# Scattering the first three batches' rows in groups of two instead of four, in a routed feed-forward kernel

## The chip, the cores and the metric

The kernel runs on one core of one Trainium2 chip. The metric is the device time of one launch, in microseconds (us). Names of engines: PE is TensorE, DVE is VectorE, ACT is ScalarE, POOL is GpSimd, SP is SyncE, whose queue issues most of the plain transfers.

## The reference, cut to what matters

```python
x = x + layernorm(attn(layernorm(x)))      # x is (4, 1024, 256)
x = x + layernorm(ffn(layernorm(x)))

# attn: q, k projections, rotary, exp of causal scores, row sums, then a small two-layer map
# ffn, on the 4096 rows "flat":
logits = flat @ gate_w + gate_b            # 8 experts
topv, topi = lax.top_k(logits, 2)
topw = softmax(topv)                       # two weights per row
for each expert e:                         # w1[e]: 256 x 1024, w2[e]: 1024 x 256
    h = gelu(flat @ w1[e] + b1[e])
    final += (h @ w2[e] + b2[e]) * routing[:, e]
```

Every row goes to two of eight experts. The kernel computes only those two.

## The kernel before, in words

The attention part works batch by batch, four batches (B) of 1024 rows. While batch j + 1 is in the attention part, batch j is routed: the gate's logits, the two best experts and each row's place are computed (`choose`, `rank`, `place_rows`), and the rows are scattered into a DRAM table `sorted_x`, in which each expert has a region of its own. Rows lie on 128 partitions, 8 tiles (TB) to a batch, and each goes to two experts, so a batch is sent by 16 indirect transfers of 128 rows of 260 floats (133 KB) each. `send_rows` (L190, the transfer on L195) issues them on POOL, and every one adds 16 to the semaphore `rows_sent`.

After the attention part come the tiles of 256 rows of one expert each: SP loads a tile `xt` from `sorted_x`, PE turns it, multiplies it by the first layer (L838 for the tiles worked ahead, L1638 in the main loop), ACT takes the GELU, DVE splits the result in two parts, PE does the second layer (L845, L1651), and POOL adds the rows to the DRAM sum `sum_y` (L542). Matrices are split in a high and a low part, so each product is three matmuls.

What sets the order around the change:

- POOL's program is in order. For the batches 0 to 2 it waits for `rows_ready` of that batch (given by DVE, L1161), issues the 16 transfers in groups of `BURST`, waits (`hold`, L75) before each further group until all the ones ahead have landed, and after the last group waits for its landing too, and gives `rows_left` (L569 to L575). The last batch (L580 to L587) is sent in portions that are a list of its own, `SEND_FIRST`, between the additions to `sum_y` of the first two tiles.
- SP's queue issues the weights of the first two experts as soon as the busiest expert is known (L524 to L530, 4 transfers of 1 MB), and then waits until batches 0 and 1 are wholly landed, `rows_sent` at 2 batches (L531), and loads the first two tiles (L536). These are worked ahead, amid the last batch's attention part.
- PE's program has `turn_ahead(0)` (L824, which waits for the first tile) ahead of `attention_mlp(3)` (L806, L815) and of the first layer of that tile (L838). Before `turn_ahead(0)` stand 14 matmuls of `keep_warm` (L748), which compute nothing that is used. DVE too has `save_tag(0)` (L473), which waits for the first tile, ahead of `hidden(3)` (L1012 to L1021).
- Every later tile waits until batches 0 to 2 have landed, and some until all four have (L1487).
- DVE waits for `rows_left` of batch 0 at L1155 (batch 2's places) and L1334, and for that of batch 1 at L1155 (batch 3's places) and L1359.

Of the kernel before, what the change touches and what calls it, by code (L numbers as in the profile page):

```python
# [58 lines left out]
SP_ENDS = 4  # L59
END_SENT = NE * 16  # L60
SEND_FIRST = (6, 8, 11)
BURST = 4


RSQRT_LINKS = 8
# [9 lines left out]
def hold(eng, sem, value, passed):  # L75

    eng.wait_ge(sem, value)
    eng.sem_inc(passed, 1)
# [48 lines left out]
def build(nc, x_in, wqT, wkT, fc1_w, fc1_b, fc2_wT, fc2_b, low_rows, gate_w, gate_b, w1, b1T, w2, b2,  # L127
# [7 lines left out]
    with ExitStack() as ctx:  # L135
# [54 lines left out]
        def send_rows(pool, c, which):  # L190

            rows = xrow_last if c == B - 1 else xrows[:, c * TB:(c + 1) * TB, :]
            for i in which:
                at = c % 2 * 2 * TB + i
                pool.indirect_dma_start(  # L195
                    out=sorted_x, out_offset=bass.IndirectOffsetOnAxis(ap=slot_i[:, at:at + 1], axis=0),
                    in_=rows[:, i % TB, :], in_offset=None).then_inc(rows_sent, 16)
# [350 lines left out]
        def _(pool):  # L548
# [20 lines left out]
            for b in range(B - 1):  # L569
                pool.wait_ge(rows_ready, b + 1)  # L570
                for first in range(0, 2 * TB, BURST):
                    if first > 0:
                        hold(pool, rows_sent, b * BATCH_SENT + first * 16, passed)
                    send_rows(pool, b, range(first, first + BURST))
                hold(pool, rows_sent, (b + 1) * BATCH_SENT, rows_left)  # L575
# [1287 lines left out]
```

## Time and profile before

| | |
|---|---|
| median of 3 runs | 625.47 us (624.44 to 625.89) |
| the profiled execution, its own time | 628.62 us |
| its span, first to last instruction | 626.8 us |
| PE busy | 559.9 us (89%) |
| DVE busy | 415.6 us (66%) |
| ACT busy | 366.1 us (58%) |
| POOL busy | 182.6 us (29%) |
| mean granted clock of TensorE | 0.982 of full speed |

The busy shares are averages over a program with two unlike parts: up to about 195 us the attention part and the routing, from there to about 603 us the loop over expert tiles, in which PE is nearly always busy. Times in the rows below are counted from the span's start. The indirect transfers show twice: the instruction on POOL that issues one (about 1 us of POOL), and its landing, which shows only in who waited for it.

### The profile page before, as it was taken

How to read it: one execution, taken by the hardware profiler on the slowest of the kernel's cores; microseconds unless marked ns; L12 is line 12 of the kernel's file. 1: busy time of each engine (PE TensorE's matmuls, PEld its weight loads, DVE VectorE, ACT ScalarE, POOL GpSimd, SP SyncE). 2: the span in 40 equal slices, each digit the busy share in tenths (PEclk: the TensorE clock that was granted, in tenths of full speed). 3: DMA queues.
4: the chain of work that ended last, by engine and by line, in shares of the span. 5: the costliest groups of instructions: out<-in, count | busy, mean ns of one | idle time of the engine just before them, and what ended most of it. 6: DMA issues, size and time to landing. Idle time of an engine off the chain costs nothing.

```text
span 626.8 us, 14745 instructions
## 1 busy us (share of the span) xinstructions
PE 559.9 (89%) x4306; PEld 499.4 (80%) x4307; DVE 415.6 (66%) x1293; ACT 366.1 (58%) x836; POOL 182.6 (29%) x153
## 2 busy tenths in 40 slices
PE   2988998987998899999999999899999999999940
PEld 1747373644668899999999989899999999998940
DVE  4789698987987555455554556486489655455476
ACT  4376677774644453644635565684688654553582
POOL 2000054355536622313214213113212312312320
PEclk9999999999999989999999999999999999999985
DMA  8930011633227732323322263473473422322479
GB/s 221 359 127 0 2 69 69 237 136 111 73 101 191 225 51 51 50 34 54 47 43 50 43 170 61 93 244 58 70 235 81 67 36 51 50 34 51 89 201 330
DMA packets 51869, 66.80 MB, mean 107 GB/s; under 512 B 4886, under 2 KB 45308, under 8 KB 51708
## 3 DMA queue, kind: packets, MB, share of 16 engines
q1 hardware_dynamic: 37820, 47.87, 24.2%
q0 software_dynamic: 14016, 18.56, 17.2%
q8 instruction: 12, 0.20, 0.1%
q14 instruction: 21, 0.17, 0.1%
HBM read 38.26 MB, written 28.74 MB: 107 GB/s over the span
## 4 chain that ended last, share of the span: by engine, by line
PE 73%; DVE 9%; ACT 5%; issue 4%; DMA 4%; POOL 2%; another core or an unknown queue 1%; DVEq 1%; SPq 0%; ACTq 0%; POOLq 0%
PE pY L1651 30%; PE pL L1638 28%; PE pP L778 5%; DMA sorted_x<-xrows,slot_i 2%; PE pX L464 2%; DVE z L1795 2%; POOL sorted_x L195 2%; PE pP L881 2%; PE pS L795 2%; ACT probs L666 1%; PE pP L838 1%; PE pT L759 1%; ACT xn L597 1%; DMA x_all<-x 1%
## 5 line engine op out<-in xcount | busy, mean ns | idle before, releaser
L1573 ACT ACTIVATE h<-pL,b_now 128x256 f32<-128x256 f32 x272 | 112.6, 465 | 153.7 <-PE pL L1638 80.8
L542 POOL DMA_INDIRECT sum_y<-y,dest x68 | 107.0, 1573 | 274.8 <-DVE y L1695 262.4
L1668 DVE TENSOR_TENSOR h_lo<-h,h_hi 128x512 fp32r<-128x512 f32 x136 | 93.2, 692 | 112.8 <-ACT h_hi L1579 112.2
L1638 PE MATMUL pL<-xeT_hi,w_lo 128*128 128x256 f32 x544 | 151.6, 279 | 6.5 <-issue 5.7
L1651 PE MATMUL pY<-w_hi,h_lo 128*128 128x256 f32 x544 | 155.1, 285 | 2.5 <-DVE h_lo L1668 1.5
L1651 PE MATMUL pY<-w_hi,h_hi 128*128 128x256 f32 x544 | 151.6, 279 | 0.6 <-issue 0.6
L1651 PE MATMUL pY<-w_lo,h_hi 128*128 128x256 f32 x544 | 151.5, 279 | 0.5 <-issue 0.5
L1638 PE MATMUL pL<-xeT_lo,w_hi 128*128 128x256 f32 x544 | 151.0, 278 | 0.0
L1638 PE MATMUL pL<-xeT_hi,w_hi 128*128 128x256 f32 x544 | 150.9, 277 | 0.0
L1638 PEld LDWEIGHTS pL<-xeT_hi,w_lo 128*128 128x128 f32 x544 | 102.0, 188 | 7.8 <-issue 6.9
L1651 PEld LDWEIGHTS pY<-w_hi,h_lo 128*128 128x128 f32 x544 | 102.8, 189 | 4.5 <-DVE h_lo L1668 2.6
L1651 PEld LDWEIGHTS pY<-w_lo,h_hi 128*128 128x128 f32 x544 | 103.3, 190 | 0.5 <-issue 0.4
L1651 PEld LDWEIGHTS pY<-w_hi,h_hi 128*128 128x128 f32 x544 | 102.9, 189 | 0.4 <-issue 0.4
L1638 PEld LDWEIGHTS pL<-xeT_hi,w_hi 128*128 128x128 f32 x544 | 102.1, 188 | 0.1
L1638 PEld LDWEIGHTS pL<-xeT_lo,w_hi 128*128 128x128 f32 x544 | 102.1, 188 | 0.0
L1579 ACT ACTIVATE h_hi<-h 128x512 fp32r<-128x512 f32 x136 | 86.0, 632 | 6.3
L195 POOL DMA_INDIRECT sorted_x<-xrows,slot_i x48 | 49.1, 1023 | 120.0 <-DVE xrows L1161 82.3
L210 DVE TENSOR_TENSOR w_lo<-w_stage,w_hi 128x512 fp32r<-128x512 f32 x64 | 42.4, 686 | 15.0 <-issue 15.0
L1687 DVE SCALAR_TENSOR_TENSOR y<-pY,b_all 128x256 f32<-128x256 f32 x66 | 28.0, 424 | 25.4 <-PE pY L1651 25.4
L203 ACT ACTIVATE w_hi<-w_stage 128x512 fp32r<-128x512 f32 x64 | 36.8, 620 | 0.0
L1695 DVE TENSOR_SCALAR y<-y,y_mean,weight 128x256 f32<-128x256 f32 x66 | 27.6, 418 | 2.4
L617 ACT ACTIVATE qk<-pP 128x512 bf16<-128x512 f32 x32 | 19.0, 593 | 17.4 <-PE pP L778 17.2
(284 smaller groups left out, 831.8 us busy)
## 6 DMA issues: line engine op xcount, KB each, us to landing
w_stage<-w SPq DMA_DIRECT2D x16, 1024.0 KB
xt<-sorted_x SPq DMA_DIRECT2D x38, 260.0 KB
sum_y<-fill SPq DMA_DIRECT2D x1, 4352.0 KB, 20.6
w_stage<-sum_y SPq DMA_DIRECT2D x8, 512.0 KB, 6.7
out<-z SPq DMA_DIRECT2D x7, 512.0 KB, 6.4
x_all<-x SPq DMA_DIRECT2D x3, 1024.0 KB, 8.4
sorted_x<-fill SPq DMA_DIRECT2D x8, 260.0 KB
sum_y<-y,dest POOLq DMA_INDIRECT x68, 3.8
```

Of the source, the lines that this page charges most:

```text
L195: pool.indirect_dma_start(out=sorted_x, out_offset=bass.IndirectOffsetOnAxis(ap=slot_i[:, at:at + 1], axis=0), in_=rows[:, i % TB, :], in_ ...
L203: act.activation(w_hi[par][:, i, q * WQ:(q + 1) * WQ], w_stage[par][:, i, q * WQ:(q + 1) * WQ], ACT.Copy).then_inc(w_hi_ready[i], 1)
L210: low = dve.tensor_tensor(w_lo[par][:, i, piece], w_stage[par][:, i, piece], w_hi[par][:, i, piece].bitcast(F32), ALU.subtract)
L542: pool.indirect_dma_start(out=sum_y, out_offset=bass.IndirectOffsetOnAxis(ap=to[:, i:i + 1], axis=0), in_=rows[:, i, :], in_offset=None, c ...
L778: mm = pe.matmul(pP[:, n % 2, :], w[:, k, i, mo], x[:, k, tok], start=(k == 0 and w is wqk_lo), stop=(k == KC - 1 and x is xT_lo))
L1573: a = act.activation(h[:, c, :], pL[:, bk, i * TM:(i + 1) * TM], ACT.Gelu, bias=b1_now[par][:, c:c + 1])
L1579: act.activation(h_hi[:, 2 * bk:2 * bk + 2, :], h[:, 2 * bk:2 * bk + 2, :], ACT.Copy).then_inc(h_hi_ready, 1)
L1638: mm = pe.matmul(pL[:, bk, i * TM:(i + 1) * TM], w[:, 0, col], x[:, k, :], start=(k == 0 and w is lo), stop=(k == KC - 1 and x is xeT_lo))
L1651: mm = pe.matmul(pY[:, i, 0:D], s[:, c, rows], w[:, 1, c * D:(c + 1) * D], start=(c == 0 and s is h_lo), stop=(c == FC - 1 and w is lo))
L1668: dve.tensor_tensor(h_lo[:, cs, :], h[:, cs, :], h_hi[:, cs, :].bitcast(F32), ALU.subtract).then_inc(h_split, 1)
L1687: dve.scalar_tensor_tensor(out=y[:, i, :], in0=pY[:, i, 0:D], scalar=1.0, in1=b2_all[:, bass.ds(who, 1), :].rearrange("p e d -> p (e d)"), ...
L1695: dve.tensor_scalar(y[:, i, :], y[:, i, :], y_mean[:, i:i + 1], weight[:, i:i + 1], ALU.subtract, ALU.mult).then_inc(y_ready, 1)
```

## The change

```diff
 SEND_FIRST = (6, 8, 11)
-BURST = 4
+BURST = 2
```

`BURST` is used in one place (L571 to L574), which isn't itself changed:

```python
for b in range(B - 1):
    pool.wait_ge(rows_ready, b + 1)
    for first in range(0, 2 * TB, BURST):
        if first > 0:
            hold(pool, rows_sent, b * BATCH_SENT + first * 16, passed)
        send_rows(pool, b, range(first, first + BURST))
    hold(pool, rows_sent, (b + 1) * BATCH_SENT, rows_left)
```

No instruction that does work is added, removed or moved on any engine. What changes is how often POOL waits. These are POOL's rows for one of the batches 0 to 2, in the order in which the engine gets them; first before (`xrows,slot_i` is the batch's rows and the places they go to, `x3` three more of the same):

```order
L195 DMA sorted_x<-xrows,slot_i 34816x260 [waits rows_sent,rows_ready]
L195 DMA sorted_x<-xrows,slot_i 34816x260 x3
L195 DMA sorted_x<-xrows,slot_i 34816x260 [waits rows_sent]
L195 DMA sorted_x<-xrows,slot_i 34816x260 x3
L195 DMA sorted_x<-xrows,slot_i 34816x260 [waits rows_sent]
L195 DMA sorted_x<-xrows,slot_i 34816x260 x3
L195 DMA sorted_x<-xrows,slot_i 34816x260 [waits rows_sent]
L195 DMA sorted_x<-xrows,slot_i 34816x260 x3
```

And the same batch in the changed kernel, its first ten transfers:

```order
L195 DMA sorted_x<-xrows,slot_i 34816x260 [waits rows_sent,rows_ready]
L195 DMA sorted_x<-xrows,slot_i 34816x260
L195 DMA sorted_x<-xrows,slot_i 34816x260 [waits rows_sent]
L195 DMA sorted_x<-xrows,slot_i 34816x260
L195 DMA sorted_x<-xrows,slot_i 34816x260 [waits rows_sent]
L195 DMA sorted_x<-xrows,slot_i 34816x260
L195 DMA sorted_x<-xrows,slot_i 34816x260 [waits rows_sent]
L195 DMA sorted_x<-xrows,slot_i 34816x260
L195 DMA sorted_x<-xrows,slot_i 34816x260 [waits rows_sent]
L195 DMA sorted_x<-xrows,slot_i 34816x260
```

So a batch has 7 waits for a landing inside it in place of 3, and one after its last group as before: 8 in place of 4. The other engines' programs, the last batch's sends and SP's waits are the same.

## Rows read from the trace of the kernel before

**Rows 1.** The chain that ended last, 100 to 165 us: start, duration, what.

```profile
112.20 0.19 DVE xrows L1161
112.38 0.27 issue
112.65 0.97 POOL sorted_x L195
...
116.48 6.79 DMA sorted_x<-xrows,slot_i
123.26 0.02 issue
123.30 0.76 issue
...
127.90 3.24 DMA sorted_x<-xrows,slot_i
...
143.30 2.44 DMA sorted_x<-xrows,slot_i
145.75 0.05 SPq L536
...
145.90 2.59 DMA xt<-sorted_x
```

**Rows 2.** Timeline of PE: start, duration, instruction, idle time before it and its releaser.

```profile
143.19 3.19 PE L748 MATMUL pP<-cos_sb,identb 128*128 128x512 bf16 x14
148.54 0.66 PE L824 MATMUL pT<-ident,xt 128*128 128x128 f32 x4 [2.16 <-DMA xt<-sorted_x]
149.03 1.03 PE L748 MATMUL pP<-cos_sb,identb 128*128 128x512 bf16 x4
```

**Rows 3.** Timeline of POOL, batch 0.

```profile
78.35 1.06 POOL L195 DMA_INDIRECT sorted_x<-xrows,slot_i  x1 [72.74 <-DVE xrows L1161]
...
82.31 0.97 POOL L195 DMA_INDIRECT sorted_x<-xrows,slot_i  x1 [0.30 <-issue]
85.59 0.97 POOL L195 DMA_INDIRECT sorted_x<-xrows,slot_i  x1 [2.32 <-DMA sorted_x<-xrows,slot_i]
...
100.61 0.97 POOL L195 DMA_INDIRECT sorted_x<-xrows,slot_i  x1 [2.30 <-DMA sorted_x<-xrows,slot_i]
```

**Rows 4.** Timeline of POOL, end of batch 0 to the last batch.

```profile
104.43 0.97 POOL L195 DMA_INDIRECT sorted_x<-xrows,slot_i  x1 [0.30 <-issue]
112.65 0.97 POOL L195 DMA_INDIRECT sorted_x<-xrows,slot_i  x1 [7.25 <-DVE xrows L1161]
...
146.54 0.97 POOL L195 DMA_INDIRECT sorted_x<-xrows,slot_i  x1 [2.27 <-DVE xrows L1161]
...
173.75 0.97 POOL L195 DMA_INDIRECT sorted_x<-xrows,slot_i  x1 [0.30 <-issue]
182.65 0.97 POOL L195 DMA_INDIRECT sorted_x<-xrow_last,slot_i  x1 [7.93 <-DVE xrow_last L1161]
...
192.35 1.63 POOL L542 DMA_INDIRECT sum_y<-y_ahead,dest_ahead  x1 [2.21 <-DVE y_ahead L1063]
```

**Rows 5.** Timeline of DVE, its first instruction behind the wait of L1334.

```profile
136.21 1.89 DVE L210 TENSOR_TENSOR w_lo<-w_stage,w_hi 128x512 fp32r<-128x512 f32 x3
```

**Rows 6.** Stretches: busy us of each engine, granted clock, share of the DMA engines, GB/s.

```profile
78.30:85.60 7.30, 6.19 (x33) 4.22 (x33) 6.24 (x17) 5.18 (x10) 4.02 (x5) 1.00 0.21 73
...
116.00:120.00 4.00, 3.60 (x19) 2.99 (x20) 3.73 (x13) 1.90 (x4) 1.14 (x2) 1.00 0.86 315
120.00:124.00 4.00, 4.00 (x19) 3.30 (x18) 3.97 (x11) 3.54 (x12) 0.00 (x0) 1.00 1.07 404
```

**Rows 7.** Stretches around the end of the weights' transfers.

```profile
128.00:129.00 1.00, 1.00 (x9) 0.87 (x8) 1.00 (x3) 1.00 (x3) 0.87 (x1) 1.00 1.11 384
129.00:130.00 1.00, 0.46 (x5) 0.22 (x2) 0.96 (x2) 1.00 (x3) 0.00 (x0) 1.00 0.73 246
130.00:131.00 1.00, 0.17 (x2) 0.17 (x2) 0.97 (x3) 1.00 (x3) 0.00 (x0) 1.00 0.00 0
```

**Rows 8.** Stretches after PE's last matmul of the kernel.

```profile
603.00:604.00 1.00, 0.06 (x1) 0.00 (x0) 0.83 (x4) 1.00 (x6) 0.29 (x1) 1.00 0.77 248
...
606.00:607.00 1.00, 0.00 (x0) 0.00 (x0) 0.93 (x4) 1.00 (x7) 1.00 (x1) 1.00 0.76 112
607.00:608.00 1.00, 0.00 (x0) 0.00 (x0) 1.00 (x4) 1.00 (x6) 0.12 (x1) 0.78 0.56 32
608.00:609.00 1.00, 0.00 (x0) 0.00 (x0) 1.00 (x3) 0.99 (x6) 0.00 (x0) 0.50 0.70 102
```

**Rows 9.** Stretches around the only other fall of the clock.

```profile
218.00:219.00 1.00, 0.29 (x2) 0.03 (x1) 0.00 (x0) 0.00 (x0) 0.92 (x1) 1.00 0.03 4
219.00:220.00 1.00, 0.36 (x2) 0.30 (x2) 0.00 (x0) 0.71 (x2) 0.78 (x1) 1.00 0.61 63
...
222.00:223.00 1.00, 1.00 (x5) 0.71 (x4) 0.62 (x2) 0.83 (x2) 0.00 (x0) 0.50 0.46 69
...
225.00:226.00 1.00, 1.00 (x9) 1.00 (x9) 0.81 (x4) 0.00 (x0) 0.00 (x0) 0.87 0.03 8
```

**Rows 10.** The chain that ended last, 149 to 165 us.

```profile
150.91 0.67 PE pT L806 x4
...
152.25 0.74 PE pS L815 x8
153.00 7.32 PE pP L838 x48
```

**Rows 11.** Timeline of SP: its load of the third tile.

```profile
191.39 0.41 SPq L1489 DMA_DIRECT2D xt<-sorted_x  x1
```

## The prediction

> **What bounds the kernel now.** I read the page first: PE is 89% busy, and nearly all that it is not busy lies ahead of 220 us. So the question is whether POOL's sends are on the path somewhere in the attention part. The chain of work that ended last answers it. From 112.65 us on it runs through nothing but batch 1's sends: POOL issues, a landing, POOL issues, up to the landing of the 16th transfer at 143.30 + 2.44 = 145.74; then SP's load of the first tile at 145.90 [rows 1]. PE's timeline shows what stands behind it. PE ends its 14 spare matmuls at 146.38 and sits idle for 2.16 us until the tile is there [rows 2]; `attention_mlp(3)`, the tile's first layer and all the rest are queued behind that. DVE has its copy of the tile's tag ahead of `hidden(3)`, so it waits too. Hence a us by which batch 1 lands later is a us at the end, with no slack to eat first. Batch 0 matters only if it runs into batch 1, batch 2 only if it runs into the last one.
>
> Then POOL's timeline, for the price of one wait. In batch 0 the transfers of one group start 1.28 us apart (0.97 to 1.06 of POOL's time and 0.30 of idle), and between groups POOL is idle 2.30 us [rows 3]. That idle time is the last transfer's own way to DRAM: it lands 2.44 us after its issue began, 1.47 us after POOL is done with it, and POOL restarts 0.76 us (and some hundredths) after the landing [rows 1]. It isn't a backlog of four: in that stretch the DMA engines were busy 0.21 of the time, 0.21 x 7.3 = 1.5 us for a group that takes 5.1 us to issue [rows 6].
>
> **The change part by part.** Each batch gets 4 more waits. Each puts 2.30 us where there were 0.30: **+2.0 us a wait, +8.0 us a batch**. Nothing else is issued.
>
> *Batch 0.* It begins at 78.35 as before. Before, POOL was done with its last transfer at 104.43 + 0.97 = 105.40, and free at 107.7 with the landing; batch 1's rows were ready for a start at 112.65, so 4.95 us were slack [rows 3, 4]. Now it is free at 107.7 + 8.0 = 115.7. So batch 1 starts **3.05 us** later. DVE comes to its first wait for batch 0's landing at 136.2 [rows 5], 20 us after that: nothing.
>
> *Batch 1.* Before it took from 112.65 to 145.74. Its first two groups met the 4 MB of weights, with the DMA engines at 1.07 and 404 GB/s [rows 6]: the first group landed 6.79 us after its last issue, the second 3.24 us, in place of 2.44 [rows 1]. The weights were through between 129 and 130 us [rows 7]. What four extra waits cost in that stretch no row shows, so I bound it. *Low*: no contention is left in the new kernel, all eight pairs take 1.28 + 0.97 + 2.30 = 4.55 us, and the last lands at 115.7 + 36.4 - 0.8 = 151.3, which is +5.6. *High*: the first pair sees the full 6.79 (1.28 + 6.79 + 0.76 = 8.8, to 124.5), the second, which would begin when the second group did before, is released when that was, at 131.94, and six clear pairs follow: 131.9 + 27.3 - 0.8 = 158.4, or +12.7. *Taken*: the excess stays as it is, for 4 transfers now cross the loaded stretch in two pairs as 4 to 7 did before in two groups. Then batch 1 lands 3.05 + 8.0 = **+11.05** late, at 156.8. A working by backlog says about the same: three transfers that met the load took from about 115.5 to 123.27 - 1.47 = 121.8, 2.1 us each; two pairs at that rate are over at 130.5, and six clear ones end at 157.0.
>
> A rule that speaks of this: the Trainium skill (DMA: Bandwidth & Descriptors, "Queues, rings and completion order") says that each DMA engine serves its queues in turn, packet by packet, so that a small transfer need not wait for a long one's end. By it a 133 KB transfer would share with as much or, where the weights' rows are 4 KB against its 1 KB, four times as much of theirs: an estimate of 1.6 us a transfer at 404 GB/s in place of my 2.1, and a delay 1.6 us smaller. The row of 6.79 us is slower than that rule makes it, and I go by the row.
>
> *What is behind the tile.* PE, idle 2.16 us before, will be idle about 13.2 us (from 146.4 to 159.6). The rows show what such idleness does: after PE's last matmul of the kernel, at 603.06, the granted clock stood at 1.00 up to 607 and was 0.50, 1.2 GHz, from 608 on [rows 8]; and after a few thin microseconds at 218 to 220 it was 0.50 from 222 until 225, with PE busy [rows 9]. So PE comes back at 1.2 GHz. What is first there is the tile's transposes and four spare matmuls (1.5 us at full clock), `hidden(3)`'s transposes (0.67 us), the spare two and the eight of L815 (0.74 us), then L838 [rows 2, 10]. In [rows 9] the low clock lasted 3 to 4 us of busy PE, during which a matmul took twice the time, so half of it, 1.5 to 2 us, was lost. Bounds: 0 (the clock is kept, or the loss lies beside DVE's and ACT's parts of the chain) and 3.2 (6.4 us low, as long as it takes in the rows from 148.54 to beyond L815's end with a matmul or two of L838). I take **+2.0**, near the row of the same kind.
>
> *Batch 2.* Its rows are ready as before, at about 146.3, since DVE gives them ahead of its wait for the tile; POOL begins it when batch 1 is through, at 157.6, and it takes 30.5 + 8.0 (before: 146.54 to 173.75 + 0.97 + 2.3 = 177.0 [rows 4]), to 196.1. The last batch would begin at 182.65 + 13.05 = 195.7. So POOL is 0.4 us late, and it has 2.21 us of idle time before the first addition to `sum_y` to hide that [rows 4]. **0.** The cover goes if batch 2 needs 1.8 us more than this. SP's load of the third tile needs batch 2 landed, but it came at 191.39, 15 us after that landing was over [rows 11].
>
> Sum: 3.05 + 8.0 + 2.0 + 0 = **+13.05 us**. The profiled execution took 628.62 us, 3.15 over the median; the sum is made in its times and is a difference, so I put it on the median: 625.47 + 13.05 = **638.5 us**. In the profiled execution's own terms: 641.7.
>
> **The rivals.** *(a) Waits that shrink with the group: no loss.* If the time to a landing were the backlog of the whole group, a pair would wait 1.15 us and the eight waits cost what four did, while four gaps of 0.30 go: 1.2 us less in batch 1, batch 0's part hidden; 624.3 us, inside the 0.2% of 625.5 (1.25 us, about what this kernel's measurements can tell) or just past it. It decides in favour of faster as soon as a pair's wait is under 1.3 us. For it: the first loaded group's 6.79 us is backlog. Against it: the 0.21 of busy DMA engines, and a last group that waits 2.44 us with all ahead of it long drained. 3%.
>
> *(b) Loaded pairs each pay the full 6.79 us.* Batch 1 at +12.7, the rest as forecast, POOL 2 us late into batch 2 and the cover nearly gone: 625.5 + 12.7 + 2.0 to 2.5 = 640.5 us. For it: latency under load need not depend on how many are in the queue. 20%.
>
> *(c) The load is over sooner, or weighs little on pairs.* Batch 1 at +5.6 to +9, clock +2.0: 633.1 to 636.5. For it: fewer rows compete in the same stretch, and the packet rule above. 18%.
>
> *(d) The clock costs nothing that shows.* 625.5 + 11.05 = 636.5. For it: PE had waits for DVE and ACT in that stretch. 15%.
>
> *(e) The change doesn't reach the path.* The order of POOL's program shows the waits, and SP waits for the count they hold up. 1%: 625.5.
>
> **How the numbers follow.** The forecast, with the two terms of 11.05 and 2.0 within a microsecond or so, gets 43%. Together the cases of a loss hold 96%. The range reaches from 633.5 (the middle of (c)'s lower part) to 642.5 ((b) with a clock term of 3.2 and some lateness of POOL): what lies outside is (a), (e), the lowest of (c) and a highest case in which everything costs its upper bound, 18% in all. Faster 1%, the same 3%, slower 96%.
>
> **What would show each step.** In the changed kernel's trace: 21 waits inside the three batches in place of 9, with idle times of 2.3 us before every second L195; the first of batch 1 at 115.7; the first tile's load at about 157; an idle PE of 13 us ahead of L824 and a granted clock of 0.50 there and for some microseconds after; L838's start, 153.0 before, at about 166; from 195 us on the same program, shifted. The prediction is wrong if pairs wait 1.3 us (then (a)), if the tile's load moves by much less than 11 us (then (c)), or if the loop from 200 us on isn't just shifted.

## The result

| | before | changed |
|---|---|---|
| median | 624.96 us (4 runs, 624.36 to 625.89) | 638.09 us (4 runs, 635.03 to 641.07) |
| profiled execution, its own time | 628.62 us | 638.64 us |
| its span | 626.8 us | 636.8 us |
| mean granted clock of TensorE | 0.982 | 0.967 |
| first tile's load (L536) | 145.90 us | 161.11 us |

The ratio is 1.022, 95% interval 1.0188 to 1.0253: slower by 11.7 to 15.8 us, 13.1 by the medians. The forecast was 638.5. The two numbers agree better than their workings do: the chain up to the first tile's load lost 4 us more than forecast, and what lies behind the first tile took that back. The profiled execution of before was 3.7 us over its median, that of the changed kernel 0.6, so the two traces differ by 10.0 us only.

The page of the changed kernel, its first lines and the granted clock in 40 slices:

```profile
span 636.8 us, 14757 instructions
...
PE 556.0 (87%) x4306; PEld 496.3 (78%) x4307; DVE 413.9 (65%) x1293; ACT 365.2 (57%) x836; POOL 184.3 (29%) x153
...
PEclk9999999996799999999999999999999999999985
```

PE, DVE and ACT work no more than before, POOL 1.7 us more (184.3 in place of 182.6). The granted clock has a new hole at 143 to 175 us. What grew is waiting. This is the view of who waited for whom, 100 to 240 us, of the changed kernel (us in total, times, longest us):

```profile
POOL sorted_x L195 <- DMA sorted_x<-xrows,slot_i: 55.8, 20, 6.2
...
PE pT L824 <- DMA xt<-sorted_x: 19.0, 1, 19.0
DVE tag L473 <- DMA xt<-sorted_x: 18.3, 1, 18.3
```

POOL waited 20 times in that stretch for a landing, 55.8 us. PE waited 19.0 us for the tile, where it had waited 2.16 [rows 2]. POOL's timeline of the changed kernel (columns as in [rows 3]):

```profile
77.42 1.06 POOL L195 DMA_INDIRECT sorted_x<-xrows,slot_i  x1 [71.82 <-DVE xrows L1161]
...
82.33 0.97 POOL L195 DMA_INDIRECT sorted_x<-xrows,slot_i  x1 [2.53 <-DMA sorted_x<-xrows,slot_i]
...
111.47 0.97 POOL L195 DMA_INDIRECT sorted_x<-xrows,slot_i  x1 [2.37 <-DMA sorted_x<-xrows,slot_i]
112.74 0.96 POOL L195 DMA_INDIRECT sorted_x<-xrows,slot_i  x1 [0.30 <-issue]
119.93 0.97 POOL L195 DMA_INDIRECT sorted_x<-xrows,slot_i  x1 [6.22 <-DMA sorted_x<-xrows,slot_i]
...
127.69 1.03 POOL L195 DMA_INDIRECT sorted_x<-xrows,slot_i  x1 [5.53 <-DMA sorted_x<-xrows,slot_i]
...
132.81 1.34 POOL L195 DMA_INDIRECT sorted_x<-xrows,slot_i  x1 [2.64 <-DMA sorted_x<-xrows,slot_i]
```

Eight lines that start a pair lie between 77.42 and 112.74, so 111.47 is the last pair of batch 0, and 119.93 is batch 1's first transfer. Seven waits of batch 0 were between 2.31 and 2.65 us, as [rows 3] had them. The eighth was 6.22: the pair was issued at 111.47 and 112.74, and SP's queue of the changed kernel shows what came next to it, the first two of the weights' four transfers:

```profile
112.89 0.39 SPq L180 DMA_DIRECT2D w_stage<-w  x1
113.39 0.41 SPq L186 DMA_DIRECT2D w_stage<-w  x1
...
161.11 4.41 SPq L536 DMA_DIRECT2D xt<-sorted_x  x2
```

Batch 0 took 42.5 us (77.42 to 119.93) where it had taken 29.35. Batch 1 took 41.0 us (119.93 to its last landing, 158.36 + 2.58 = 160.94) where it had taken 33.1. The chain that ended last, of the changed kernel, behind that:

```profile
158.36 2.58 DMA sorted_x<-xrows,slot_i
...
161.11 2.69 DMA xt<-sorted_x
...
163.85 1.12 PE pT L824 x4
...
169.04 2.50 DVE mstats L118 x4
```

The four transposes took 1.12 us where they had taken 0.66 [rows 2]. The stretches of the changed kernel around them show why (columns as in [rows 6]):

```profile
148.00:150.00 2.00, 0.00 (x0) 0.00 (x0) 0.00 (x0) 0.00 (x0) 1.69 (x2) 0.56 0.18 67
...
164.00:165.00 1.00, 1.00 (x5) 0.85 (x6) 0.90 (x5) 0.00 (x1) 0.00 (x0) 0.50 0.37 133
...
168.00:170.00 2.00, 2.00 (x16) 1.56 (x16) 0.96 (x2) 1.74 (x4) 0.78 (x1) 0.82 0.38 133
```

PE's last spare matmul ended at 144.88; the clock was at 1.2 GHz from the stretch 148 to 150 on and came back within 168 to 170. The matmuls of L815 began 7.20 us after the tile's load was issued (168.31 against 161.11), before 6.35 [rows 1, 10]: 0.85 us more. The matmuls between lost more than that to the low clock, but before PE had idle time in front of L806, and in the changed kernel that is filled. PE's timeline, first before, then changed:

```profile
150.91 0.66 PE L806 MATMUL pT<-ident,hid 128*128 128x128 f32 x4 [0.86 <-DVE hid L1021]
```

```profile
166.46 1.06 PE L806 MATMUL pT<-ident,hid 128*128 128x128 f32 x4
```

### The profile page after: what moved, and what is told of

It is laid out like the page before. It is cut to its first block, busy times and chain, and to the rows that moved or that the text cites. A ratio compares the mean times of both kernels' runs of the same rounds, so it can differ in the third digit from the quotient of the medians.

```text
span 636.8 us, 14757 instructions
## 1 busy us (share of the span) xinstructions
PE 556.0 (87%) x4306; PEld 496.3 (78%) x4307; DVE 413.9 (65%) x1293; ACT 365.2 (57%) x836; POOL 184.3 (29%) x153
## 4 chain that ended last, share of the span: by engine, by line
PE 63%; DMA 11%; DVE 9%; issue 7%; POOL 4%; ACT 4%; DVEq 1%; POOLq 0%; SPq 0%; ACTq 0%
PE pY L1651 27%; PE pL L1638 25%; DMA sorted_x<-xrows,slot_i 8%; POOL sorted_x L195 3%; PE pP L778 3%; PE pX L464 2%; DVE z L1795 2%; DMA sum_y<-y,dest 2%; PE pS L795 1%; PE pP L881 1%; POOL sum_y L542 1%; DMA xt<-sorted_x 1%; ACT probs L666 1%; ACT xn L597 1%; ACT z L1810 1%
## 5 line engine op out<-in xcount | busy, mean ns | idle before, releaser
L1573 ACT ACTIVATE h<-pL,b_now 128x256 f32<-128x256 f32 x272 | 112.3, 464 | 150.5 <-PE pL L1638 145.4
L542 POOL DMA_INDIRECT sum_y<-y,dest x68 | 108.3, 1592 | 267.2 <-DVE y L1695 255.5
L1638 PE MATMUL pL<-xeT_hi,w_lo 128*128 128x256 f32 x544 | 151.5, 278 | 6.9 <-issue 5.8
L1638 PE MATMUL pL<-xeT_lo,w_hi 128*128 128x256 f32 x544 | 150.8, 277 | 0.0
L1638 PE MATMUL pL<-xeT_hi,w_hi 128*128 128x256 f32 x544 | 150.6, 277 | 0.0
L1638 PEld LDWEIGHTS pL<-xeT_hi,w_lo 128*128 128x128 f32 x544 | 102.1, 188 | 8.2 <-issue 7.0
L1638 PEld LDWEIGHTS pL<-xeT_lo,w_hi 128*128 128x128 f32 x544 | 102.1, 188 | 0.0
L1638 PEld LDWEIGHTS pL<-xeT_hi,w_hi 128*128 128x128 f32 x544 | 102.1, 188 | 0.0
```

The source lines that it names most:

```text
L542: pool.indirect_dma_start(out=sum_y, out_offset=bass.IndirectOffsetOnAxis(ap=to[:, i:i + 1], axis=0), in_=rows[:, i, :], in_offset=None, c ...
L1573: a = act.activation(h[:, c, :], pL[:, bk, i * TM:(i + 1) * TM], ACT.Gelu, bias=b1_now[par][:, c:c + 1])
L1638: mm = pe.matmul(pL[:, bk, i * TM:(i + 1) * TM], w[:, 0, col], x[:, k, :], start=(k == 0 and w is lo), stop=(k == KC - 1 and x is xeT_lo))
```

## The experiments

Each is timed against runs of the kernel before on the same chip: 624.82 us in the first four experiments, 629.05 in the second four, 629.27 in the last four. So ratios are to be compared across groups, not times. The ratios and their intervals are those of the measurement; they differ a little from the quotients of the medians given beside them. For the tile's load I use the times of the traces as they stand; four traces whose program is the same up to there gave 145.90, 145.28, 145.97 and 145.94, mean 145.8.

### One batch at a time

The group's size was made a list by batch in three kernels:

```diff
-BURST = 4
+BURST = (4, 2, 2)      # batch1_and_2_in_twos
+BURST = (2, 4, 4)      # batch0_in_twos
+BURST = (4, 4, 2)      # batch2_in_twos
...
-                for first in range(0, 2 * TB, BURST):
+                for first in range(0, 2 * TB, BURST[b]):
...
-                    send_rows(pool, b, range(first, first + BURST))
+                    send_rows(pool, b, range(first, first + BURST[b]))
```

Batches 1 and 2 in twos:

> Batch 0 in groups of four again, batches 1 and 2 in twos. Theory (a wait costs 2.0 us, and the overrun of batch 0 cost 8 us because its last pair met the weights): batch 1 starts within a few tenths of rows ready, 112.7; its first two pairs meet the weights with waits of about 6 us, six follow at 4.6 us; the first tile's load comes at about 156, 10.4 us later than in the kernel before; time 635 to 636 us. Rival (the waits of batch 1 are all that matters, what batch 0 does is absorbed): the same as the changed kernel, tile load at 161 and 638 us.

Measured: 637.21 us, ratio 1.0209 (1.0171 to 1.0247). The starts of its batch 1 on POOL, and the tile's load on SP's queue:

```profile
111.68 0.97 POOL L195 DMA_INDIRECT sorted_x<-xrows,slot_i  x1 [6.50 <-DVE xrows L1161]
...
120.98 0.97 POOL L195 DMA_INDIRECT sorted_x<-xrows,slot_i  x1 [7.07 <-DMA sorted_x<-xrows,slot_i]
...
128.74 0.97 POOL L195 DMA_INDIRECT sorted_x<-xrows,slot_i  x1 [5.51 <-DMA sorted_x<-xrows,slot_i]
...
133.42 1.47 POOL L195 DMA_INDIRECT sorted_x<-xrows,slot_i  x1 [2.45 <-DMA sorted_x<-xrows,slot_i]
```

```profile
156.98 4.71 SPq L536 DMA_DIRECT2D xt<-sorted_x  x2
```

The load came 11.2 us after the mean of the four, the forecast of this run was 10.4. Its time is 1.2 us above the 635 to 636 that were expected. Two pairs met the weights and paid 7.07 and 5.51 us. From batch 1's start to the tile's load this kernel took 45.3 us, the two profiles of the kernel before 33.3 and 33.7: here batch 1 alone cost about 12 us and not 8.0, since in fours two groups pay for the load, only one of them in full (6.62 and 3.07 us).

Batch 0 in twos:

> Only batch 0 in groups of two. Theory: batch 1 starts at about 120 in place of 112.7, since batch 0's last pair waits 6 us under the weights; its first group still meets their end (wait about 5 us), the other three go at 7.1 us; the tile's load at about 151, 5.5 us late; time 630 to 631 us. Rival (what batch 1 loses by starting late it wins back because the weights are through): tile load within 3 us of 145.9, time under 628 us.

Measured: 628.94 us, ratio 1.0094 (1.0057 to 1.0131). The trace of this kernel, POOL and SP's queue:

```profile
111.49 0.97 POOL L195 DMA_INDIRECT sorted_x<-xrows,slot_i  x1 [2.28 <-DMA sorted_x<-xrows,slot_i]
...
116.33 0.96 POOL L195 DMA_INDIRECT sorted_x<-xrows,slot_i  x1 [2.60 <-DMA sorted_x<-xrows,slot_i]
...
127.76 1.75 POOL L195 DMA_INDIRECT sorted_x<-xrows,slot_i  x1 [6.65 <-DMA sorted_x<-xrows,slot_i]
...
135.90 0.97 POOL L195 DMA_INDIRECT sorted_x<-xrows,slot_i  x1 [2.33 <-DMA sorted_x<-xrows,slot_i]
```

```profile
113.92 0.39 SPq L180 DMA_DIRECT2D w_stage<-w  x1
...
150.62 4.85 SPq L536 DMA_DIRECT2D xt<-sorted_x  x2
```

In this execution the weights were issued at 113.92, 1 us later than in the changed kernel, and batch 0's last pair, issued at the same time as there, got through just ahead of them (2.60 us). So batch 1 began at 116.33 and not at the expected 120, and its first group then met nearly all of the weights. The load was 4.8 us late, and the time 4.1 us longer by the medians, 3.6 to 8.2 by the ratio's interval. So the rival, that a late start is won back, is out for groups of four: batch 1 began 4.5 us later than in the four traces (mean 111.86), and none of that came back. For pairs it holds by half. The changed kernel began batch 1 8.25 us later than batch1_and_2_in_twos (119.93 against 111.68), and its tile's load came only 4.1 us later (161.11 against 156.98), since one loaded pair less was in batch 1. The two parts of the loss, 11.2 and 4.8, make 16.0, near the 15.3 of the changed kernel (161.11 against 145.8); as their starts differ, that they fit so well is in part chance.

Batch 2 in twos:

> Only batch 2 in groups of two. Theory: POOL is free at about 185 in place of 177, 2.4 us after the last batch's rows are ready; the 2.2 us of idle time ahead of the first addition to sum_y hide it but for some tenths; time 625 to 626 us. Rival (POOL's lateness goes through to the additions and the tiles): 2 us or more, 627.5 us.

Measured: 625.21 us, ratio 1.0011 (0.9991 to 1.0031). POOL's timeline of this kernel:

```profile
184.60 0.97 POOL L195 DMA_INDIRECT sorted_x<-xrow_last,slot_i  x1 [2.52 <-DMA sorted_x<-xrows,slot_i]
...
193.73 1.62 POOL L542 DMA_INDIRECT sum_y<-y_ahead,dest_ahead  x1 [1.14 <-DVE y_ahead L1063]
```

POOL came late to the last batch, and what idle time was left ahead of the first addition to `sum_y` fell from 2.21 us [rows 4] to 1.14. The cover held: no loss clear of noise, and by the interval at most 1.9 us.

### The clock

```diff
-                keep_warm(pP[:, 0, :], 5 if j < B - 2 else 14)
+                keep_warm(pP[:, 0, :], 5 if j < B - 2 else 94)
```

> The changed kernel, with 80 more of the spare matmuls ahead of the first tile's transposes (94 in place of 14, none of whose results are used), about 17 us of PE's time, which end at about the time the tile is there. Theory (the cold clock costs 0.9 us): tile load at 161 as in the changed kernel, granted clock 1.00 throughout, time 1 us under the changed kernel, 637 us. Rival (the clock costs the 2 us that were forecast, or more in later stretches): 635 to 636 us. If the spare matmuls outlast the landing by some tenths, that much is to be added.

Measured: 639.75 us, ratio 1.0240 (1.0211 to 1.0270), not faster than the changed kernel's 1.022 (1.0188 to 1.0253); both expectations fell. The stretches of this kernel say why it doesn't tell what the clock costs:

```profile
160.00:161.00 1.00, 1.00 (x7) 0.41 (x5) 0.00 (x0) 0.00 (x0) 0.00 (x0) 1.00 0.03 8
...
162.00:163.00 1.00, 0.00 (x0) 0.00 (x0) 0.00 (x0) 0.00 (x0) 0.69 (x2) 1.00 0.77 232
...
164.00:165.00 1.00, 1.00 (x5) 0.64 (x4) 0.90 (x6) 0.36 (x1) 0.00 (x0) 0.50 0.37 133
```

PE was busy to 161.57 and idle for 2.09 us, and the clock fell all the same, when the work was back. The load was at 160.82 and L815 at 167.84, 7.02 us later. The second profile of the kernel before shows that it can fall there in that kernel too:

> The kernel before, unchanged, for a second profile. Theory (the 6.6 us at 212.7 to 219.3, in which ACT waits for nothing that the profile shows, comes in some executions only, and is why the profiled execution lay 3 us over the median): the profile shows either no such wait and a time of 624 to 626, or one and 628 to 630. The tile's load at 145 to 147, and a granted clock around it that may be at either level, since two traces with the same program up to there differ in it.

Measured, with no edit: 630.42 us against 629.27, ratio 1.0012 (0.9981 to 1.0042), the profiled execution 627.63. Its tile load came at 145.28, and its timeline of PE has

```profile
148.07 1.11 PE L824 MATMUL pT<-ident,xt 128*128 128x128 f32 x4 [2.98 <-DMA xt<-sorted_x]
```

1.11 us again. The trace of batch2_in_twos, the same program up to there, was cold as well. In these two L815 began 7.03 and 7.14 us after the tile's load was issued, against 7.20 in the changed kernel. So nearly all of the 0.85 us is also paid in those executions of the kernel before in which the clock is low there, two of the four traces. The wait of ACT without a releaser is shorter in this profile: 4.15 us in front of L1573 at 218.66, where the first profile has 5.99 in front of L1573 at 219.29, and it isn't on the chain that ended last. The time, 627.63, lies between the upper bound of one case that the expectation gave and the lower bound of the other.

### What weights and rows do to each other

In two kernels the second expert's 2 MB are loaded behind the first two tiles:

```diff
             load_second(sp, e0, 0)
-            e1 = sp.value_load(busy_i[0:1, 2:3].bitcast(I32), min_val=0, max_val=NE - 1)
-            load_first(sp, e1, 1)
-            load_second(sp, e1, 1)
             sp.wait_ge(rows_sent, AHEAD * BATCH_SENT)
...
                              ).then_inc(tile_in, 16)
+            e1 = sp.value_load(busy_i[0:1, 2:3].bitcast(I32), min_val=0, max_val=NE - 1)
+            load_first(sp, e1, 1)
+            load_second(sp, e1, 1)
             sp.wait_ge(ends_ready, 1)
```

> The changed kernel, with the 2 MB of the second expert's weights loaded behind the loads of the first two tiles, in place of ahead of them: the sends of batches 0 and 1 meet half the weights. Theory (what the overrun of batch 0 cost above its waits, and part of batch 1's, is that pairs meet the weights, 6 us a pair in place of 2.3): the loaded stretch shrinks from about 13 us to about 6, one pair or two pay in place of two or three, the first tile's load comes at 155 to 158 in place of 161, time 632 to 635 us. Rival (a pair is slowed by something else that falls there, as PE's or DVE's work): load at 161, 638 us.

Measured, in twos: 642.75 us against 629.05, ratio 1.0233 (1.0197 to 1.0270). POOL's timeline of this kernel:

```profile
116.06 0.97 POOL L195 DMA_INDIRECT sorted_x<-xrows,slot_i  x1 [3.03 <-DMA sorted_x<-xrows,slot_i]
...
123.29 0.97 POOL L195 DMA_INDIRECT sorted_x<-xrows,slot_i  x1 [4.99 <-DMA sorted_x<-xrows,slot_i]
...
127.82 0.97 POOL L195 DMA_INDIRECT sorted_x<-xrows,slot_i  x1 [2.29 <-DMA sorted_x<-xrows,slot_i]
```

The loaded waits went from 6.22 and 5.53 us to 3.03 and 4.99, and the tile's load came at 156.40, 4.7 us sooner: the theory's half on the place is right. The time did not follow (632 to 635 us were expected). PE began the first layer (L1638) of the first tile of the main loop 4.6 us sooner than in the changed kernel, 206.62 against 211.26, but that of the third 4.3 us later, 240.97 against 236.72. The chain of this kernel holds, between 200 and 240 us, two pieces to which the profile gives no releaser; the chain of the changed kernel has none:

```profile
206.03 4.50 another core or an unknown queue
...
227.68 6.49 another core or an unknown queue
```

The same edit with groups of four:

> The kernel before, with the second expert's weights loaded behind the first two tiles. Theory: the first group of batch 1 still meets weights, the second doesn't; the tile's load comes 1 to 4 us sooner, of which 1 to 2 us can reach the end: 623 to 624.5 us. Rival (the late weights then slow the second tile's load, batch 2 and the words of the plan): 625 us or more.

Measured: 625.36 us against 629.05, ratio 0.9959 (0.9935 to 0.9983), a small gain clear of noise. Its groups behind the weights waited 5.94 and 2.75 us (6.62 and 3.07 in POOL's timeline of the kernel before), the tile's load came at 144.57, and PE had the tile 1.79 us after it asked. The load came 1.2 us sooner than the mean of the four; the gain by the ratio is 2.6 us (1.1 to 4.1), so it isn't shown that all of it comes from there. It is faster than both kernels.

### Longer groups

```diff
-BURST = 4
+BURST = 8      # eights; (8, 4, 4) in batch0_in_eights
```

> Groups of eight in batches 0 to 2: one wait inside a batch in place of three. Theory (2.0 us a wait, and no slack behind batch 1 but 1 to 2 us): the sends of batch 1 end 4 us sooner, the tile's load comes at about 142, but PE is busy to 146.4 and DVE to 147.5 whatever the tile does, so only 1 to 2 us of it reach the end: 623 to 624 us. Rival (the loss and the gain are symmetric): 621 us. Rival (eight in flight pile up): waits of more than 4 us in the unloaded stretch, and no gain.

Measured: 639.81 us against 629.05, ratio 1.0185 (1.0145 to 1.0225). All three expectations fell: it is almost as slow as groups of two, and not by longer landings. Its batch 1 begins at 116.19 and is loaded as a tile at 144.76, 28.6 us where the second profile of before has 145.28 - 111.56 = 33.7, so the waits it lacks did give 5 us. But rows were ready 4.6 us later (115.91 against 111.28), those of batch 2 9.3 us later (153.81 against 144.55), and PE came to the tile, whose load had been issued 0.5 us sooner, only at 154.18, with no wait for it, 6.1 us later than in the second profile of before:

```profile
154.18 0.60 PE L824 MATMUL pT<-ident,xt 128*128 128x128 f32 x4
```

The wait table of this kernel, 60 to 240 us, shows a kind that the changed kernel hasn't ("remote" is a releaser that the profile doesn't know):

```profile
ACT h L688 <- remote: 5.4, 1, 5.4
ACT qk L617 <- remote: 4.3, 1, 4.3
ACT h L1573 <- remote: 4.0, 1, 4.0
```

> Batch 0 in groups of eight, batches 1 and 2 in fours. Theory (eight in flight stall the engines' own streams, some 5 us a batch, and that is what made the kernel of eights 11 us slower): waits of ACT or PE with no releaser between 78 and 105, weights issued at about 117 in place of 113, the tile's load at about 150, no such wait later; 629 to 630 us. Rival (the loss of the eights came from batch 1 meeting the weights alone): 625 us, no change.

Measured: 637.45 us against 629.27, ratio 1.0106 (1.0050 to 1.0162), 6.7 us by the ratio; 629 to 630 us were expected, that is, a loss of some 5 us. PE's timeline, a stretch, POOL's timeline and SP's queue of this kernel:

```profile
87.79 0.47 PE L778 MATMUL pP<-xT_hi,wqk_lo 128*128 128x512 f32 x1 [1.83 <-issue]
```

```profile
104.00:106.00 2.00, 1.88 (x4) 0.39 (x4) 0.00 (x0) 1.20 (x4) 0.00 (x0) 0.50 0.00 0
```

```profile
118.33 0.97 POOL L195 DMA_INDIRECT sorted_x<-xrows,slot_i  x1 [18.72 <-DVE xrows L1161]
```

```profile
119.61 0.38 SPq L180 DMA_DIRECT2D w_stage<-w  x1
```

The weights were issued at 119.61 and the tile's load came at 151.54, 5.7 us late, with batch 1 in fours. The delay is there before batch 1 starts: PE has idle time of 1.83 us without a releaser in front of one projection, the clock falls to 0.50 twice between 88 and 106, and everything up to the plan of batch 1 is 6 to 7 us late. In all three kernels with batch 0 in eights the rows of batch 1 were ready at 115.9 to 118.1, in the eleven others at 110.8 to 112.4. The rival, that only the weights matter, is out. The waits without releaser that the expectation named are there in part only (1.83 us on PE; later two of 2 us), so what exactly delays the engines is left open: the engines' own streams of instructions come by DMA too (queues q8 and q14 of the page), and their waiting behind rows would look like this, but no row ties one to the other.

> Groups of eight and the second expert's weights late, both. Theory: the tile is there before PE and DVE ask for it, so its wait is gone; nothing above the 1 to 2 us of either: 622.5 to 624 us. If the two gains add, 621 us.

Measured: 641.07 us against 629.05, ratio 1.0183 (1.0150 to 1.0216). The two edits together are no better than eights alone.

### The last batch

```diff
-            send_rows(pool, B - 1, range(SEND_FIRST[2], 2 * TB))
+            send_rows(pool, B - 1, range(SEND_FIRST[2], SEND_FIRST[2] + 2))
+            hold(pool, rows_sent, (B - 1) * BATCH_SENT + (SEND_FIRST[2] + 2) * 16, passed)
+            send_rows(pool, B - 1, range(SEND_FIRST[2] + 2, 2 * TB))
```

> The kernel before, and the last five sends of the last batch as two and three, with a wait for the landing between them (one more wait on POOL). Theory (the wait of ACT without releaser at 212 to 220 comes from many transfers in flight): it is gone in every profile, and the median falls by the share of executions that have it, less up to 2.0 us for the wait where POOL is what the tiles wait for: 623 to 627 us. Rival (that stall has nothing to do with those sends): it is still there in some, 625 to 629 us.

Measured: 633.03 us against 629.27, ratio 1.0057 (1.0025 to 1.0088), slower by 3.6 us. POOL's timeline of this kernel at the new wait:

```profile
218.66 2.29 POOL L195 DMA_INDIRECT sorted_x<-xrow_last,slot_i  x1 [3.52 <-DMA sorted_x<-xrow_last,slot_i]
```

The new wait is 3.52 us, and it is in front of the additions to `sum_y`, for which DVE waits. The long wait without releaser isn't on this profile's chain at 212 to 220, but with one profile, and one of two profiles of the kernel before without it on its chain as well, that shows nothing.

> The second expert's weights late, as in fours_second_weights_late, and the last five sends in two parts. Theory: the two don't touch; if the stall goes, 2 to 4 us below the kernel before of the same chip. Rival: POOL's extra wait costs 2 us and eats the gain, equal to the kernel before.

Measured: 630.76 us against 629.27, ratio 1.0009 (0.9983 to 1.0035): the extra wait eats the gain of the late weights, as the rival said.

## Why the prediction was right, and where its terms were not

**The place.** Batch 1's sends lead the chain up to the first tile, and PE has no slack behind them. Right: PE's wait for the tile went from 2.16 to 19.0 us, and the load is 15.3 us later.

**A wait costs 2.0 us.** Right, in the unloaded stretch: idle times of 2.27 to 2.65 us for nearly all. Batch 1's term of 8.0 us measured 41.0 - 33.1 = 7.9, but that it came out so exactly is luck: started on time, batch 1 in twos cost about 12 us (batch1_and_2_in_twos), and only the late start let it miss part of the weights.

**"So batch 1 starts 3.05 us later."** This step failed. Batch 1 started at 119.93, where its rows were ready for a start at 111.7 (batch1_and_2_in_twos), 8.2 us late. I had put the end of batch 0 at 115.7 and, in the working by backlog, the start of the load at about 115.5, and did not lay one over the other: batch 0's last pair was still on its way when the weights came, and waited 6.22 us in place of 2.3. That is 3.9 of the missing 5.2; the rest are waits and issues a tenth or two longer. batch0_in_twos shows that it is a matter of a microsecond: there the pair slipped through. The last landing of batch 1 came 15.2 us late (160.94 against 145.74), above the 11.05 that I took and above the 12.7 that I had called the high bound, which let the overrun of batch 0 be 3.05 us in every case.

**The excess under load.** I took it as unchanged. With the late start the first pair of batch 1 paid 3.2 us over a clear wait (5.53), and two later ones 0.3 and 0.9 (2.64 and 3.23); before, the groups of four paid 4.3 and 0.8. So for batch 1 it was nearly so. Rival (b), that a pair under load waits as long as a group of four, had the mechanism right: 6.22, 5.53, 7.07 and 5.51 us for pairs, 6.62 for four. The working by backlog doesn't fit: it gave 2.1 us a transfer, and the first pair of batch1_and_2_in_twos took 9.3 us (111.68 to 120.98), 4.7 a transfer. The packet rule of the Trainium skill (DMA: Bandwidth & Descriptors, "Queues, rings and completion order") made loaded waits cheaper still than I did; here they were dearer, 4.8 to 7.1 us (4.76 in twos_pe_kept_busy) where a clear wait is 2.3.

**Clock +2.0.** Too large: 0.85 us, and under 0.2 us against those traces of the kernel before in which the clock is low there too. Its direction and the 0.50 in the rows were right. What was left out is PE's own idle time in front of L806, 0.86 us before, which took up part of what the matmuls lost. The high bound's 6.4 us at the low clock is more than its rows hold, 4.5 us from 148.54 to the end of L815 (152.25 + 0.74). The rival (d), that the clock costs nothing that shows, was nearer in this term.

**Batch 2: 0.** Right, by its own experiment.

**The sum.** To the first tile's load 15.3 against 11.05; then 0.85 against 2.0; by that the end should be 16 us late, and the medians say 13.1 (11.7 to 15.8). I had written that from 195 us on the program is just shifted. It isn't. This is how late the changed kernel's trace is against the two profiles of before, in us:

| | against the first | against the second |
|---|---|---|
| first tile's load issued | 15.2 | 15.8 |
| PE's first layer (L1638), first tile of the main loop | 14.3 | 14.4 |
| the same, fourth tile | 11.7 | 13.5 |
| the same, fourteenth tile | 11.7 | 13.3 |
| the same, last tile | 10.0 | 10.7 |

Against the first profile 2.6 us come back between the first and the fourth tile, where it has waits without a releaser (6.56 us on its chain at 212.7) and the changed kernel has none; against the second, where ACT's is 4.15 us and off the chain, only 0.9. The 1.7 to 2.6 us that come back between the fourteenth tile and the last are there against both, so that wait doesn't explain them. Why they come wasn't settled. So the forecast's time was right partly by luck: errors of opposite sign met, 4 us too little ahead of the tile against 1 us too much for the clock and some 3 us that came back behind it and stood in no term.

**Rival (a)**, waits that shrink with the group, is out with the 2.3 us of pairs; (c), a batch 1 that lands less than 9 us late, is out with the 15.2; (e) is out.

## What to carry to other kernels

A wait for a landing costs the last transfer's own way (here 2.3 us in place of 0.3), whatever the number sent ahead of it, so smaller groups cost by their count; and where the chain runs through the sends there is nothing to hide that. When a change makes one stretch longer, lay its new end over every other engine's transfers near it: the biggest error here was a pair that ran into 4 MB of weights by less than 2 us. And the opposite edit isn't the opposite gain: eights saved the waits and lost 1.85%, so a group's size is to be measured on both sides.

## What the runs showed that I had not expected

- The time to a landing under load hardly depends on how many transfers the group has. POOL waited 4.8 to 7.1 us for pairs and 6.4 to 7.1 for the first group of four; with half of the weights 3.0 and 5.0 for pairs and 5.9 for a group of four.
- A late start of the sends cost in full with groups of four (4.5 us late, load 4.8 us late) and by half with pairs (8.25 us late, load 4.1 us late).
- With more indirect transfers in flight, engines whose programs are unchanged came late: batch 0 in eights put the rows of batch 1 from 111.3 to 118.05 and the weights' issue from 113 to 119.6, and cost 1.06% (0.50 to 1.62%). By which way isn't shown.
- The clock fell after 2.09 us of idle PE in one kernel and stood at 1.00 after 2.16 us in another [rows 2], at the same place of the program.
- Moving 2 MB of weights behind the first two tiles gained 0.41% (0.17 to 0.65%) with groups of four, and nothing with groups of two, where it brought the tile's load 4.7 us forward.
